# Linear attention: four of sixteen key-value products move to GpSimd, their values spread by a store and a load

## The reference, cut to what matters

```
q = x @ Wq.T;  k = x @ Wk.T * SCALE;  v = x @ Wv.T;  gproj = x @ Wg.T + bg
gk = log_sigmoid(x @ Wkg1.T @ Wkg2.T + bkg2) / 16
def step(S, inp):                      # over the 256 tokens of a batch row
    S = S * exp(gt)[..., None] + kt[..., None] * vt[..., None, :]
    ot = einsum('bhk,bhkv->bhv', qt, S)
o = normalise(ot);  y = silu(gproj) * o @ Wo.T
```

## Time and profile before

| | before |
|---|---|
| median of 3 runs | 645.79 us (644.98 to 646.8) |
| the profiled execution | 648.34 us |
| its span, from the first to the last instruction | 646.5 us |
| TensorE, VectorE, ScalarE, GpSimd busy | 545.7, 329.2, 224.3, 353.0 us |
| granted TensorE clock, mean | 0.918 |

### The profile page before, as it was taken

How to read it: one execution, slowest core, us unless ns; L and a number is a source line. 1 busy time by engine, 2 the same in 40 slices (tenths; PEclk the granted TensorE clock), 3 DMA queues, 4 the chain that set the end, 5 groups by cost and what they waited for, 6 DMA issues and landing times.

```text
span 646.5 us, 9617 instructions
## 1 busy us (share of the span) xinstructions
PE 545.7 (84%) x3085; PEld 445.6 (69%) x3085; DVE 329.2 (51%) x726; ACT 224.3 (35%) x526; POOL 353.0 (55%) x316
## 2 busy tenths in 40 slices
PE   8899865149999996639898877797999999999995
PEld 4666664138888885628664435785888888888885
DVE  4645786504665432212379895667333323335365
ACT  4645442104555763312350201432222222222233
POOL 3473115777578886550027876016484585759190
PEclk9979997578999997768898996998999999999999
DMA  8999882334667665430000006100333423423221
GB/s 258 374 386 386 286 271 74 108 121 120 190 201 220 207 183 175 119 97 24 0 1 1 1 0 189 31 2 7 106 93 98 146 99 98 122 79 115 61 65 66
DMA packets 72866, 83.71 MB, mean 129 GB/s; under 512 B 7618, under 2 KB 63699, under 8 KB 72819
## 3 DMA queue, kind: packets, MB, share of 16 engines
q1 hardware_dynamic: 33490, 38.90, 19.9%
q10 hardware_dynamic: 35968, 35.26, 16.3%
q0 software_dynamic: 3360, 8.93, 4.4%
HBM read 48.61 MB, written 34.47 MB: 128 GB/s over the span
## 4 chain that ended last, share of the span: by engine, by line
PE 63%; DVE 13%; issue 7%; DMA 4%; ACT 2%; another core or an unknown queue 2%; ACTq 1%; POOL 0%; DVEq 0%
PE PS L1841 45%; DMA FA<-xg 4%; PE PS L2065 2%; DVE FA L1797 2%; DVE PS L1779 2%; PE PS L2183 2%; PE PS L2207 1%; PE PS L2294 1%; PE PS L1916 1%; PE PS L1938 1%; PE PS L2108 1%; PE PS L2078 1%; PE PS L2306 1%; DVE HC L1553 1%
## 5 line engine op out<-in xcount | busy, mean ns | idle before, releaser
L1841 PE MATMUL PS<-XH,EW 128*128 128x512 f32 x400 | 133.2, 398 | 0.1
L1841 PEld LDWEIGHTS PS<-XH,EW 128*128 128x128 f32 x400 | 76.0, 190 | 16.6 <-DVE EW L1200 0.6
L1569 DVE TENSOR_TENSOR FA<-OGATE,PS 128x512 f32<-128x512 f32 x42 | 28.9, 688 | 110.8 <-ACT OGATE L1008 94.6
L1841 PE MATMUL PS<-EW,XH 128*128 (+2 forms) x252 | 79.8, 401 | 6.1 <-issue 4.7
L1841 PE MATMUL PS<-XL,EW 128*128 128x512 f32 x200 | 79.1, 396 | 0.0
L1008 ACT ACTIVATE OGATE<-PS 128x512 f32<-128x512 f32 x48 | 28.7, 599 | 127.8 <-PE PS L1841 127.8
L801 POOL TENSOR_TENSOR FA<-FA,QT 128x1024 f32<-128x1024 f32 (+1 forms) x16 | 37.5, 2342 | 61.2 <-DVE FA L1797 61.2
L1841 PE MATMUL PS<-EW 128*128 128x256 f32 x288 | 62.8, 283 | 0.5 <-DVE W1L L1574 0.4
L1841 PE MATMUL PS<-EW,W1L 128*128 128x256 f32 x192 | 54.3, 283 | 0.0
L1841 PEld LDWEIGHTS PS<-EW,XH 128*128 128x128 f32 x252 | 46.3, 204 | 11.3 <-issue 5.6
L1841 PEld LDWEIGHTS PS<-EW 128*128 128x128 f32 x288 | 49.4, 190 | 4.0 <-DVE W1L L1574 1.2
(11 more groups left out here) (385 smaller groups left out, 1278.9 us busy)
## 6 DMA issues: line engine op xcount, KB each, us to landing
xg<-EQ ACTq DMA_DIRECT2D x1, 16384.0 KB, 61.0
EG<-in_gateup SPq DMA_DIRECT2D x16, 448.0 KB, 4.0
yg<-EQ ACTq DMA_DIRECT2D x1, 6016.0 KB, 20.3
FA<-xg ACTq DMA_DIRECT2D x47, 128.0 KB
yg<-FA ACTq DMA_DIRECT2D x47, 128.0 KB, 1.9
ED<-in_down SPq DMA_DIRECT2D x16, 224.0 KB, 4.7
EG<-in_gateup SPq DMA_DIRECT2D x16, 192.0 KB
FA<-in_gateup SPq DMA_DIRECT2D x16, 192.0 KB, 3.0
```

Of the source, the lines that this page charges most:

```text
L1569: dve.tensor_tensor(mixed[:, i % MIXED, :], sil_t[:, i % 2, :], bank(step_bank(i) + 1), ALU.mult).then_inc(mixed_dve, 1)
L1841: ins = pe.matmul(o, l, r, start=start and i == 0, stop=stop and i == n - 1, skip_group_check=True)
```

## The change

The products of v = 5, 7, 10 and 13 go from VectorE to GpSimd. GpSimd can't read PSUM, so these values don't come by TensorE: the value rows are put together in fp32 (values 0 to 7 by an addition of high and low part on GpSimd ahead of the loop, values 8 to 15 by two copies on ScalarE), SP stores the 16 rows of one v to DRAM with each repeated 8 times (512 KB), waits, and loads the result back on 128 partitions (512 KB) into one of two SBUF rooms in `HC`. GpSimd multiplies there by `KT`, and VectorE's scan reads that room. The product of v stands behind the query product of v-3. The five pieces of the first quad's split move behind the loop. The diff (the renamed semaphores `cleared`, `rooms_zero` and `room_stored` left out):

```diff
+        POOL_VALUES = (5, 7, 10, 13)
+        DVE_VALUES = tuple(v for v in range(DV1) if v not in POOL_VALUES)
+        kv_room = [HC[:].rearrange("p t d -> p (t d)")[:, j * T:(j + 1) * T] for j in range(2)]
+        values_f = [kv_room[1], OT[:, 1, :]]
...
             load_gate(0)
             load_down(0)
+            for j, v in enumerate(POOL_VALUES):
+                if j % 2 == 0:
+                    sp.wait_ge(values_ready, j // 2 + 1)
+                r = v % 8 * NH1
+                sp.dma_start(value_room[j], values_f[v // 8][r:r + NH1, :].unsqueeze(1).broadcast_to([NH1, DK1, T])
+                             ).then_inc(room_stored, 16)
+                sp.wait_ge(room_stored, 16 * (j + 1))
+                if j >= 2:
+                    sp.wait_ge(s_done, POOL_VALUES[j - 2] + 1)
+                sp.dma_start(kv_room[j % 2], value_room[j].rearrange("h k t -> (h k) t")
+                             ).then_inc(spread_ld[j % 2], 16)
             sp.wait_ge(s_done, DV1)
...
-            g, gh, gl, d, dh, dl = quad_slot(0)
+            pool.wait_ge(vt_lo, 2)
+            pool.tensor_tensor(values_f[0], VTH[:, 0, :].bitcast(F32), VTL[:, 0, :].bitcast(F32), ALU.add
+                               ).then_inc(values_ready, 1)
             for v in range(DV1):
...
-                if v == 1:
-                    pool.wait_ge(gate_ld[0], 32 * KD)
-                    g_rounded = high(gh, g, whole)
...
-                if v == 9:
-                    low(dl, d, dh, whole, d_rounded).then_inc(down_split, 1)
...
+                if v + 3 in POOL_VALUES:
+                    j = POOL_VALUES.index(v + 3)
+                    pool.wait_ge(spread_ld[j % 2], 16 * (j // 2 + 1))
+                    pool.tensor_tensor(kv_room[j % 2], KT, kv_room[j % 2], ALU.mult).then_inc(kv_pool, 1)
+
+            for q in range(2):
+                g, gh, gl, d, dh, dl = quad_slot(q)
+                pool.wait_ge(gate_ld[q], 32 * KD)
+                g_rounded = high(gh, g, whole)
+                low(gl, g, gh, whole, g_rounded).then_inc(gate_split, 1)
+                pool.wait_ge(down_ld[q], 16)
+                d_rounded = high(dh, d, whole)
+                low(dl, d, dh, whole, d_rounded).then_inc(down_split, 1)
...
+            act.wait_ge(values_ready, 1)
+            for hf in range(2):
+                act.wait_ge(vt_mm, 3 + hf)
+                ins = act.activation(values_f[1][:, halves[hf]], bank(6 + hf), ACT.Copy)
+            ins.then_inc(values_ready, 1)
             value_hi(1, 6)
...
             for v in range(DV1):
-                if v > 0:
+                if v > 0 and v in DVE_VALUES:
                     kv_product(v)
...
+                if v in DVE_VALUES:
+                    n = DVE_VALUES.index(v)
+                    dve.wait_ge(d1_done, n + 1)
+                    kv = spread_v(n)
+                else:
+                    j = POOL_VALUES.index(v)
+                    dve.wait_ge(kv_pool, j + 1)
+                    kv = kv_room[j % 2]
                 if v >= 2:
                     dve.wait_ge(qs_done, v - 1)
+                dve.tensor_tensor_scan(STATE[:, v % 2, :], DEC, kv, 0.0, ALU.mult, ALU.add).then_inc(s_done, 1)
...
-                if v >= 2:
-                    pe.wait_ge(s_done, v - 1)
+                n = DVE_VALUES.index(v)
+                s = n % 2
+                if n >= 2:
+                    pe.wait_ge(s_done, DVE_VALUES[n - 2] + 1)
...
-                    spread(v + 2)
+                if v + 2 in DVE_VALUES:
+                    spread(v + 2)
```

More of the change, by code:

```diff
@@ L83, in build_kernel @@
         yg = nc.dram_tensor("yg", (SLOT_TILES * P, D), F32).ap()
+        value_room = nc.dram_tensor("value_room", (len(POOL_VALUES), NH1, DK1, T), F32).ap()
         cw_room = nc.dram_tensor("cw_room", (E1, T), F32).ap()
@@ L290, in build_kernel @@
         stored = sem("stored")
-        zb_set = sem("zb_set")
+        cleared = sem("cleared")
         ones_set = sem("ones_set")
@@ L383, in build_kernel @@
         d1_done = sem("d1_done")
+        kv_pool = sem("kv_pool")
+        values_ready = sem("values_ready")
         s_done = sem("s_done")
@@ L388, in build_kernel @@
         qs_used = sem("qs_used")
[L389 to L390 removed]
+        rooms_zero = sem("rooms_zero")
         mask_ready = sem("mask_ready")
@@ L605, in _ @@
             sp.wait_ge(cw_step, CW_COPIED)
-            sp.dma_start(cw_room, cw_turned).then_inc(cw_stored, 16)
-            sp.wait_ge(cw_stored, 16)
+            sp.dma_start(cw_room, cw_turned).then_inc(room_stored, 16)
+            sp.wait_ge(room_stored, 16 * (len(POOL_VALUES) + 1))
             for i in range(STEPS):
@@ L683, in _ @@
             chained = ch.n - 6
-            pool.wait_ge(xg_zero, 16)
+            pool.wait_ge(rooms_zero, 16)
             def scatter(t, k):
@@ L863, in _ @@
                         pool.wait_ge(mixed_dve, v - AHEAD + 1)
-                    pool.wait_ge(spread_ld[v % SPREADS], 32 * (v // SPREADS + 1))
+                    pool.wait_ge(spread_ld[v % SPREADS], 32 * (v // SPREADS + (2 if v % SPREADS < 2 else 1)))
                     pool.tensor_tensor(mixed[:, v % MIXED, :], mixed[:, v % MIXED, :], spread_w[v % SPREADS], ALU.mult
@@ L1191, in _ @@
             ch = Counter(dve, dve_chain)
-            dve.memset(zb[:], 0.0).then_inc(zb_set, 1)
-            dve.memset(EQ[:], 0.0).then_inc(zero_set, 1)
+            dve.memset(zb[:], 0.0).then_inc(cleared, 1)
+            dve.memset(EQ[:], 0.0).then_inc(cleared, 1)
             for k in range(KD):
@@ L1793, in _ @@
                     value_lo(1, 6)
-                dve.wait_ge(d1_done, v + 1)
+                if v in DVE_VALUES:
[6 more added lines that the diff above has]
+                    kv = kv_room[j % 2]
                 if v >= 2:
                     dve.wait_ge(qs_done, v - 1)
-                dve.tensor_tensor_scan(STATE[:, v % 2, :], DEC, spread_v(v), 0.0, ALU.mult, ALU.add
-                                       ).then_inc(s_done, 1)
+                dve.tensor_tensor_scan(STATE[:, v % 2, :], DEC, kv, 0.0, ALU.mult, ALU.add).then_inc(s_done, 1)
             for c in range(2):
@@ L1855, in ws @@
                 return [(wh[:, k, c:c + n], wl[:, k, c:c + n]) for k in range(KD)]
-            pe.wait_ge(zb_set, 1)
+            pe.wait_ge(cleared, 1)
             def keep_warm(n, b):
@@ L2355, in _ @@
             for v in range(DV1):
-                if v + 2 < DV1:
-                    if v + 2 == DV1 // 2:
-                        pe.wait_ge(vt_lo, 4)
+                if v + 2 == DV1 // 2:
+                    pe.wait_ge(vt_lo, 4)
+                if v + 2 in DVE_VALUES:
                     spread(v + 2)
```

20 lines of the change are left out of this document (10 added, 10 removed).

## The result

The changed kernel takes 659.56 us (median of 6 runs, 657.0 to 664.36), the kernel before 646.29 us (6 runs, 644.06 to 650.87). The ratio is 1.0205, with a 95% interval of 1.0168 to 1.0243: **13.3 us slower**. The forecast was 654.1 us, range 648 to 661, slower with a chance of 0.8. Direction and range hold; the loss is 5 us larger than the forecast of 8.3 us.

The account below looks back on a forecast made before the run. The loop ended with VectorE before; after the change GpSimd's lane was to bound it. Loop 6.3 us later plus 2 us behind it made 8.3 us, on 645.8 us giving 654.1 us; range 648 to 661 us.

Parts of the forecast that it names:

- The port: In the loop, four scans with two SBUF inputs and GpSimd exclude each other for the whole scan: 8.0 us.
- Rival (a): In the loop, the scan shares the port and isn't shut out: 644.3 us, or 642.4 with short stores; chance 0.20.
- The transfers: Stores 7.0 us (bounds 5.3 to 11.4), loads 4.2 us; GpSimd waits 3.6 us for the first room.
- Rival (b): Stores take 11.4 us, so GpSimd waits for every room in the loop: 660 to 662 us; chance 0.10.
- The loop: Linear attention's loop, with GpSimd's lane as the bound, ends 6.3 us later: 399.85 against 393.5 us.
- the walk: Instruction-by-instruction calculation of the loop from its first product, using traced durations and the code's waits; gave 393.5 us before.
- gather 13: Late in the loop GpSimd waits 1.2 us for this gather, behind TensorE's spread 15 and residual.
- Behind the loop: GpSimd's longer splits meet the head scaling, with two SBUF inputs: 2 us, range 0 to 4.2 us.
- The clock: TensorE's granted clock may fall in the loop's longer gaps: taken as 0, with 2.4 us kept for the range.
- the 7 us saved on VectorE: In the loop, four products (5.0 us) and spread waits (about 2 us) leave VectorE's lane, if nothing else changed.

Follow-up runs that it names:

- experiments 2: Changed kernel, but the four scans read the preceding column's PSUM bank, leaving the four moved products out of the result: 656.4 us, ratio 1.0139 to the kernel before.
- 7: Changed kernel with first quad's split ahead of the loop, v = 6, 8, 11, 14 on GpSimd, products copied to PSUM by ScalarE: 645.98 us, ratio 0.9974 to before.
- experiment 9: Changed kernel with first quad's split ahead of the loop and v = 6, 8, 11, 14 on GpSimd, scans reading the rooms: 613.52 us, ratio 1.0114 to before.
- experiment 4: Changed kernel without the values' stores and loads, GpSimd multiplying what the rooms hold: 656.94 us, ratio 1.0167 to the kernel before.
- experiment 5: Changed kernel with each spread's four matmuls done twice on TensorE: 663.37 us, ratio 1.0253 to the kernel before.
- experiment 8: Kernel before with only the first quad's split moved ahead of the loop: 649.28 us, ratio 0.9998 to the kernel before.
- Experiment 1: Kernel before with only the first quad's split moved behind the loop, all products on VectorE: 650.43 us, ratio 1.0046 to the kernel before.
- Experiment 6: Changed kernel with the first quad's split ahead of the loop instead of behind it: 657.06 us, ratio 1.0171 to the kernel before.
- Experiment 3: Changed kernel, but GpSimd waits with both quads' splits until the head scaling is done: 657.58 us, ratio 1.0155 to the kernel before.
- 10: Changed kernel, split ahead, only v = 8, 11, 14 on GpSimd, ScalarE copying products to PSUM, no GpSimd addition: 603.61 us, ratio 0.9924 to before.

## Why the prediction was right, and where its sizes were off

**The port: right.** The forecast was a hold for the whole scan, in which GpSimd does nothing and for which the scan waits. The four scans show 4.36 us, GpSimd stands for 2.23 us through each of the last three, and experiments 2, 7 and 9 switch the effect on and off with the scan's input. 7 and 9 differ besides only in ScalarE's copies and the order of the banks; their four scans take 2.28 and 4.36 us. One thing was told too simply: GpSimd stands there mostly for the scan's result, which comes late because the scan waited; in the changed profile only the product at 353.05 us was held with nothing else to wait for, by some 1.3 us, and in experiments 4, 5 and 9 the ones named there. The sum is the same: 3 x 2.23 + 1.3 = 8.0 us, the forecast's figure. Rival (a) fell. The Trainium skill (SBUF — State Buffer, Who interferes with whom) words the condition for any VectorE instruction with two SBUF inputs beside a GpSimd instruction that reads SBUF; the traces agree for the scan, 4.36 against 2.29 us.

**The transfers: right within the bounds.** 7.1 and 7.3 us for the stores where 7.0 was taken, 3.9 us for the loads where it was 4.2. GpSimd waited 3.41 us before the first room (forecast 3.6) and 0.70 us before the second. Rival (b) fell. Experiment 4 puts stores and loads at 2.5 us.

**The loop: +4.7 us in the profile, forecast +6.3.** GpSimd's last full query product ended 63.76 us after the first product, where the walk had 64.54 us: 0.8 us less. The last gather took 1.05 instead of the 2.0 us assumed, 0.95 us less. These make the difference. One term had the right size and the wrong wait: the 1.2 us that the forecast gave to gather 13 were 1.08 us for the scan of v = 14. And the 63.12 us of the profile before hold the slow stretch of 1.5 us that experiment 8 is free of; against a loop without it the loss would be larger.

**Behind the loop: +5.7 us, forecast +2 (0 to 4.2).** This is the term that failed. Three pieces, from the stage table: up to the start of the head scaling 11.63 instead of 9.78 us (+1.85), the head scaling 5.20 instead of 2.77 us (+2.43), from its end to the first statistics 4.55 instead of 3.10 us (+1.45, a wait of 1.89 us for TensorE's output projection). The third piece isn't the splits themselves: experiments 1, 4 and 5, with both quads split behind the loop, have 3.1 us there. In the changed profile TensorE waited 1.65 us within the longer head scaling, the granted clock was 0.70 in 414 to 418 us, and the four matmuls of the residual at 414.26 us (L2133) took 1.91 us; in 1 and 4 they took 1.03 us at a granted clock of 1.00. The head scaling alone lay inside the range given. What was not charged to the splits at all is the square of the last half (L1809 before, L1834 now), which the forecast doesn't name: it too has both inputs in SBUF, runs on the chain just behind the last gather, and met the 3.42 us split: 3.62 instead of 0.69 us. Of these 2.93 us the start of the head scaling shows 1.85. The prediction looked for what the splits would meet at the end of their stretch, and not at its start. Experiment 1 gives the splits' own size: 3.5 us of tail in the profile (19.19 against 15.65 us; 4 has 19.19 us as well) and 3.0 us in the runs. That it lies inside 0 to 4.2 us is luck, since that range was worked out from the head scaling alone. Experiment 6 brings back 5.3 us of tail, and 2.2 us in the runs, within their noise. Experiment 3 shows that waiting instead moves most of it.

**The clock: taken as 0; open.** Loop and tail make 4.7 + 5.7 = 10.4 us of the 10.5 us by which the changed profile is longer behind the first product. (Ahead of it, where only the profiled runs differ as far as the rows show, it is 1.8 us shorter: 328.62 against 330.41 us; hence 8.7 us for the span.) The median says 13.3 us. Runs of one kernel differ by about 1% with the mean granted clock (the changed kernel: 657.0 us at 0.917, 664.4 at 0.895), and both profiles were not typical of their kernels, in opposite directions. So some 2.8 us of the median lie in runs without a trace. That the gaps the change makes in TensorE's work lower the clock more often fits this, but was only argued: experiment 5 was meant to show it and did not. What single slow stretches cost the rows do show: 1.56 us between the loops of 1 and 8, 1.45 us behind the head scaling, and late in the loops of 3 and 4 some 4 us. Such stretches are of the size of what is missing, and nothing in the forecast's term of 0 stood for them.

**Where the 7 us saved on VectorE went.** The aim could be met in small part only. With the product copied to PSUM, VectorE's last scan ends 56.74 us after the first product, against 57.73 us in the control 8: of the 5.0 us of products taken off VectorE 1.0 us is left, mainly since it then waits 4.0 us for TensorE's spreads and 1.1 us before the scans, where the control waits 1.1 and 0.5 us. Part of this may be the clock: three spreads of 7 took 1.83 to 2.08 us, in 8 none took more than 1.21 us.

## What to carry to other kernels

Before work goes from VectorE to GpSimd, list for every VectorE instruction beside it whether both its inputs lie in SBUF; one such instruction stops GpSimd for its length and waits for what GpSimd has begun. If the moved work's result is what VectorE reads next, the move itself makes such an instruction; a copy into PSUM by an idle ScalarE (two of 0.59 us here) can buy it off. And work that is moved off a loop must be laid against the first instructions behind the loop as well as the last: what was hidden beside PSUM readers isn't hidden beside the first short SBUF instruction of the next stage. Last, set a stage's length against a control that has everything but the one change: of the 3.4 us by which 7 seemed to shorten the loop, 1.5 us vanish against control 8 and 0.9 us are one gather at another clock.

## What the runs showed of the hardware

- A scan with two SBUF inputs holds GpSimd out as an elementwise instruction does: 4.36 us when issued into a running 2.37 us product, 2.27 us when issued 0.16 us ahead of it (the query product then took 4.28 us, experiment 4). With one input from PSUM it takes 2.29 us beside the same work.
- Behind the loop, the 128x512 square took 3.62, 2.75 or 0.69 us as the long split beside it had begun 0.35 us ahead of it (changed), 1.22 us ahead (1) or was not running (before).
- The hold doesn't shrink with the instruction: one of 128x8 elements took 2.98 instead of 0.17 us (experiment 3).
- A group of four spread matmuls took 1.20 us at a granted clock of 1.00 and 2.07 us in a stretch at 0.63 to 0.80; in two like loops that alone made 1.56 us (1 and 8).
- A waiting scan went ahead of GpSimd's next instruction even where that one was ready (experiment 9, 311.67 us, the one case on record): the hold changed hands between instructions.
- A DMA of 16 partitions with each row read eight times (512 KB) took 7.1 to 7.3 us, the same bytes back onto 128 partitions 3.9 us.
- Three chips gave 646.8, 647.5 and 606.3 us for the same kernel before. The difference of 40 us lay ahead of this loop: 7 and 10, on two of the chips, took 312.37 and 312.33 us from the loop's first product on. What makes it isn't shown.
